# Later loads in the pair attention of layers 1 and 3: when a unit's queries and keys are fetched

## What is computed

```python
h = jnp.concatenate([x, latents], axis=1)
q = (latents @ q_w + q_b).reshape(b, k_len, NH, DH)
kv = (h @ kv_w + kv_b).reshape(b, p + k_len, NH, DH, 2)
kmat, v = (kv[..., 0], kv[..., 1])
attn = jnp.einsum('bkhd,bnhd->bhkn', q, kmat) / DH
attn = jnp.where(full_mask[:, None, None, :], attn, -jnp.inf)
attn = jax.nn.softmax(attn.astype(jnp.float32), axis=-1)
attn_out = jnp.einsum('bhkn,bnhd->bkhd', attn, v).reshape(b, k_len, H)
```

## Time and profile before

| what | value |
|---|---|
| runs | 1387.09, 1380.42, 1385.77 us; median 1385.77 |
| the profiled execution's own time | 1387.44 us |
| its span, first to last instruction | 1385.6 us |
| mean granted TensorE clock | 0.932 of full speed |
| PE busy | 1224.4 us, 88% of the span |
| DVE busy | 991.2 us, 72% |
| ACT busy | 724.4 us, 52% |
| layer 1's pair attention, first score product | 777.48 us from the span's start |
| layer 3's pair attention, first score product | 1189.88 us |

### The profile page before, as it was taken

How to read it: one execution, slowest core, us unless ns; L and a number is a source line. 1 busy time by engine, 2 the same in 40 slices (tenths; PEclk the granted TensorE clock), 3 DMA queues, 4 the chain that set the end, 5 groups by cost and what they waited for, 6 DMA issues and landing times. The chain is left out here.

```text
span 1385.6 us, 27506 instructions
## 1 busy us (share of the span) xinstructions
PE 1224.4 (88%) x9162; PEld 1010.4 (73%) x9162; DVE 991.2 (72%) x2232; ACT 724.4 (52%) x1644; POOL 496.1 (36%) x649
## 2 busy tenths in 40 slices
PE   4799999999599999999599699969599976599969
PEld 4699999999599999998588455559377756455558
DVE  5688778887588887887773689465488866589464
ACT  3466656666366665666542177541166642177441
POOL 2754555444274445542150000030199950000030
PEclk8899999999899999999899789979799998699979
DMA  4111111010210111010013875020660014874020
GB/s 151 47 31 32 32 30 30 23 30 0 95 37 26 31 31 30 10 36 0 31 65 56 133 82 61 13 77 1 190 138 2 2 51 86 108 83 55 13 65 31
DMA packets 56609, 70.91 MB, mean 51 GB/s; under 512 B 7340, under 2 KB 49118, under 8 KB 54178
## 3 DMA queue, kind: packets, MB, share of 16 engines
q1 hardware_dynamic: 55420, 66.40, 22.7%
q10 hardware_dynamic: 1086, 3.20, 0.9%
HBM read 46.79 MB, written 8.13 MB: 40 GB/s over the span
## 5 line engine op out<-in xcount | busy, mean ns | idle before, releaser
L804 ACT ACTIVATE a_prob<-a_s_ps,a_negmax 128x257 f32<-128x257 f32 x256 | 119.2, 476 | 92.3 <-DVE a_negmax L894 92.3
L1864 DVE TENSOR_REDUCE s_mx<-s_s_ps 128x2 f32<-128x1024 f32 x128 | 151.9, 1211 | 17.8 <-PE s_s_ps L1909 17.6
L1849 ACT ACTIVATE s_probT<-s_st_ps 128x512 f32<-128x512 f32 x256 | 132.1, 605 | 59.9 <-PE s_st_ps L1923 57.5
L743 POOL TENSOR_TENSOR x_v_hi<-a_v_sum,x_one 128x512 fp32r<-128x512 f32 x60 | 63.2, 1054 | 242.5 <-DVE a_v_sum L883 242.4
L368 POOL MEMSET r_power<- 128x8 f32 x3 | 0.3, 105 | 362.7 <-POOLq L1976 329.3
L1653 POOL TENSOR_SCALAR s_below<-s_masked,s_mx 128x256 f32<-128x256 f32 x256 | 118.6, 485 | 27.9 <-DVE s_mx L1681 27.8
L909 DVE TENSOR_TENSOR a_pT_lo<-a_t_ps,a_pT_hi 128x512 fp32r<-128x512 f32 x128 | 88.2, 689 | 35.9 <-ACT a_pT_hi L817 34.2
L894 DVE TENSOR_REDUCE a_negmax<-a_s_ps 128x2 f32<-128x514 f32 x128 | 86.9, 688 | 26.0 <-PE a_s_ps L951 24.2
L1681 DVE CUSTOM_DVE_ANT_0 s_masked<-s_s_ps,l_mask 128x256 f32<-128x256 f32 x256 | 90.7, 421 | 15.5 <-PE s_s_ps L1718 15.5
L817 ACT ACTIVATE a_pT_hi<-a_t_ps 128x512 fp32r<-128x512 f32 x128 | 76.7, 600 | 47.3 <-PE a_t_ps L1005 44.1
L1666 ACT ACTIVATE s_probT<-s_st_ps 128x512 f32<-128x512 f32 x128 | 69.7, 595 | 28.3 <-PE s_st_ps L1728 28.3
(11 more groups left out here) (272 smaller groups left out, 4068.4 us busy)
## 6 DMA issues: line engine op xcount, KB each, us to landing
x_wqk_raw<-L_xattn_wq SPq DMA_DIRECT2D x32, 128.0 KB, 2.3
x_wqk_raw<-L_xattn_wk SPq DMA_DIRECT2D x32, 128.0 KB, 2.2
x_wv_raw<-L_xattn_wv SPq DMA_DIRECT2D x16, 256.0 KB, 3.1
a_wo_raw<-L_xattn_wo SPq DMA_DIRECT2D x16, 256.0 KB, 3.1
l_k_st<-k_second SPq DMA_DIRECT2D x12, 256.0 KB, 9.0
l_k_st<-k_stack SPq DMA_DIRECT2D x16, 192.0 KB
l_q_st<-q_stack SPq DMA_DIRECT2D x12, 192.0 KB
x_vbias<-L_xattn_bias_v SPq DMA_DIRECT2D x2, 1024.0 KB, 4.7
```

What stands on the lines that cost most here:

```text
L804: nc.scalar.activation(prob[:, n % 2, qt, 0:NK], s_ps[:, n % 2, qt, 0:NK], ACT.Exp, bias=negmax[:, n % 2, qt:qt + 1], accum_out=den[:, n % ...
L1849: nc.scalar.activation(probT[:, third % 2, n // 4, n // 2 % 2, n % 2], st_ps[:, u % 3], ACT.Exp, scale=c.scale).then_inc(z.exp_done, 1)
L1864: nc.vector.tensor_reduce(mx[:, i % 2, qt, a::2], s_ps[:, n % 2], AX.X, ALU.max).then_inc(z.max_done, 1)
```

## The change

Only the iteration in which each load is issued changes, and unit 1's keys are issued in two parts of three transfers (`halves`). The sizes, the number of transfers, the slots and all waits of PE stay. Within an iteration the loads still stand behind the row copies, and in iteration 7 the four constant rows stand behind the six transfers of a head.

| iteration | before | after |
|---|---|---|
| 0 | unit 1, keys (6) | none |
| 1 | unit 1, queries (6) | unit 1, keys, first half (3) |
| 2 | unit 2, head 0 | unit 1, keys, second half (3) |
| 3 | unit 2, head 1 | unit 1, queries (6) |
| 4, 5 | unit 2, heads 2, 3 | unit 2, heads 0, 1 |
| 6 | constant rows (4) | unit 2, head 2 |
| 7 | unit 3, head 0 | unit 2, head 3, then constant rows (4) |
| 8 to 10 | unit 3, heads 1 to 3 | unit 3, heads 0 to 2 |
| 11 | none | unit 3, head 3 |

```diff
-    def load(self, c, eng, is_k, dst, sem):
+    def load(self, c, eng, is_k, halves, dst, sem):
 
         stack = (self.k if is_k else self.q).rearrange("u (a s d) n -> u s d a n", s=2, d=c.HD)
-        for half in range(2):
+        for half in halves:
...
-                    if first in (0, 1):
-                        second_unit.load(c, sp, first == 0, slots[1][first == 0], unit_in[0])
-                    if first is not None and 2 <= first <= 5:
-                        late.load_head(c, sp, 2, first - 2, *slots[2], unit_in[1])
-                    if first == 6:
+                    if first in (1, 2):
+                        second_unit.load(c, sp, True, (first - 1,), slots[1][1], unit_in[0])
+                    if first == 3:
+                        second_unit.load(c, sp, False, range(2), slots[1][0], unit_in[0])
+                    if first is not None and 4 <= first <= 7:
+                        late.load_head(c, sp, 2, first - 4, *slots[2], unit_in[1])
+                    if first == 7:
                         constant_rows()
-                    if first is not None and 7 <= first <= 10:
+                    if first is not None and 8 <= first <= 11:
                         sp.wait_ge(z.st_done, NE * B)
-                        late.load_head(c, sp, 3, first - 7, *slots[0], unit_in[2])
+                        late.load_head(c, sp, 3, first - 8, *slots[0], unit_in[2])
```

## The result

The changed kernel takes 1425.42 us (median, 1424.08 to 1425.68), the kernel before 1386.19 us beside it: a ratio of 1.0289, 95% interval 1.0269 to 1.0309. The change costs 39 us. The profiled execution's span is 1423.9 us, 38.3 more than before, at a granted clock of 0.926 on average instead of 0.932. All instructions are the same, so only waits and the clock can have changed.

A forecast was written before the change was run, and what follows sets the result against it. TensorE, busy 88% of the span and taking instructions in order, was taken to bound the kernel. Waits of 0 + 2 x (6.8 + 5.7) = 25.0 us plus 14.6 for the clock gave 39.6, so 1426 us, own range 1419 to 1438.

The forecast's parts named there:

- Iteration 2's row early: Iteration 2, both layers: with no loads ahead, the row of maxima comes 4.7 and 5.6 us earlier, together 10.3 us gained.
- The second unit later by as much: Before iteration 4: loads end later, PE waits 4.4 us, the gain is handed back; both layers 0, bounds -4 and +3.
- The third unit: Before iteration 8: constant rows issued behind row copies and head make PE stand 6.8 us per layer, bounds 6.2 and 7.5.
- The fourth unit: Before iteration 12: head 3, issued in iteration 11, makes PE stand 5.7 us per layer, bounds 4.3 and 6.2.
- The clock: Behind the new holes TensorE runs low: 2.9 us lost for each of four long, 1.5 for two short, 14.6 in all.
- (a): Rival: PE waits as forecast, but the clock costs little, giving 1411 or 1419 us; chance 0.21.
- (b): Rival: loads land faster, only issue binds, iteration 4 keeps about 4 us; 1411, or 1400 without the clock; chance 0.07.
- (c): Rival: the row's early arrival decides, nothing new waits and the 10.3 us gain stands, 1376 us; chance 0.05.
- (d): Rival: iteration 2's gain stands and later waits add up to about the same, 1386 give or take 6; chance 0.04.
- (e): Rival: clock low 12 us after every hole and constants wait behind the head's bytes, 1442 us; chance 0.08.

The follow-up runs named there:

- full-row run: Changed kernel with 13, 34 and 20 products of 128 rows by 128 columns by 512 elements added on PE ahead of the three unit waits: 1412.58 us, ratio 1.0202.
- the two parts alone: Against the kernel before: only the second unit's loads moved as in the changed kernel, 1389.67 us; only the third and fourth units' loads one iteration later, 1421.54 us.

## Why the prediction was right

The prediction was 1426 us, the measured time is 1425.4. Step by step:

- **Iteration 2's row early.** Right in its place: there is no wait in iteration 2 any more. What the prediction left out is the next row: that of iteration 3 waits 2.7 and 2.9 us behind half the keys, so part of the gain was lost one iteration earlier than it said. It made no difference to the sum, because the bytes decide at iteration 4.
- **The second unit later by as much.** Right, and shown by the run with the queries in iteration 2. S0 of iteration 4 was put at 805.8 and came at 806.7; the two layers were put at 0 and gave +1.6, inside the bounds. That the transfers follow each other with no gap was not quite met: their share was 0.53 in 798 to 800, as the queries were only issued at 799.25. The hole itself was put at 4.4 and is 3.6 and 2.9, for the wait of iteration 3 took some of it.
- **The third unit.** This term was the most mis-sized. Between starts, S0 was due 3.24 us after the row copies of iteration 7, at 832.4, and came at 841.6: 9.2 us late, where 6.8 was said with 7.5 as the upper bound; without the clock it cost 8.7 and 8.8 us in the two layers (full-row run). Rows and head took 5.6 us (5.7 was said), but the constant rows took 4.2 us to issue behind a head (2.4 before, where only the row copies stood ahead of them), and 2.5 to land, not 1.9. The step that was mis-sized is taking the issue time of the constants from a stretch in which no head stood ahead of them in SP's queue.
- **The fourth unit.** Right: the row copies of iteration 11 went out at 864.05, so S0 was due at 864.05 + 3.24 = 867.3; it came at 872.9, 5.6 us late for a predicted 5.7. What it cost without the clock is a little less, 5.3 and 5.5 us in the run with full rows.
- **The clock.** Right in kind, and shown by the filled holes; 14.6 us were put down, 12 measured. The 8 us at the low level behind the long holes were 6.6 and 6.1 in layer 1, and what one cost was 2.0 and 2.4 us where it can be read between starts (behind the hole before iteration 8), not 2.9; behind the short hole, before iteration 4, it was 7.4 us, and 2.6 and 2.3 us of cost, where 1.5 was given. The 12 us that the prediction took as its upper bound were no like case: the kernel before was at 0.50 from 778 on, well ahead of its hole, so that hole had not lowered the clock.

So the sum is right partly by luck, since its errors cancel. Too little was put down for the third unit (3.9 us in the two layers) and for S0 of iteration 4 (1.6), too much for the fourth unit (0.6) and for the clock (2.6 by the medians). With the measured terms in their place the sum would be about 42 us, not 39.6. Against it stand the 5 to 6 us that came back at the ends of the two loops and in the last MLP, which the sum does not have.

The rivals: (a) falls, since the clock was shown to cost about 12 us, not 0 to 8; (b) by the run with early queries; (c) and (d) by the runs of the two parts alone, the one giving +5 us and the other +35; (e) put more on the clock than there was.

## What to carry to other kernels

Before loads are moved off a wait, add up for each consumer the bytes ahead of it and the issues of the queue ahead of it, for these two set two different holes here; a load that is moved "one iteration further" for the sake of another one loses exactly the iteration that hid it. What stands behind a small urgent copy has to be sized by when that copy is next needed, not pushed out as a block. And an idle hole costs its length and then the clock behind it, in this loop 2.0 to 2.6 us more (in the run with full rows, read between starts).

## What the runs showed of the hardware that was not expected

- PE being busy did not keep the clock. With 32 products of 49 rows in a hole of 8.7 us the granted clock fell to 0.50 within it; with 34 of 128 rows it stayed at 1.00, and the kernel was 0.87% faster for doing more. The kernel before shows it without any added work: PE was busy 4.00 of 4.00 us in 876 to 880 of its span and 2.00 of 2.00 in 880 to 882, and the clock was at 0.98 and then at 0.50. What it is in the work that keeps the clock was not taken apart.
- Full-row products did not bring a low clock back soon: mixed with score products and with PE busy practically throughout from 779.09 on, the granted clock was still 0.50 in 802 to 804, and came back at about 807. The Trainium skill (TensorE: Matmul & The Clock Gate, "What's actually happening") has it that a short spell of sustained work releases the clock; these rows do not agree. Why the loop's start stays low so long is left open.
- The third of four small constant copies took 2.40 us to issue behind a head's six transfers (2.34 in layer 3, 1.31 in the run with them in iteration 6), and 0.6 in the kernel before, behind the row copies alone. The transfer engines were by then at a share of 0.67 in 836 to 837 and 0.37 in 837 to 838, so it isn't their bytes alone; what holds SP there was not tried.
